# A four-layer graph network: sorted edge scopes addressed by one packed register, and fewer of them in the first streamed layer

## What is computed

```python
h = jnp.maximum(_layernorm(x), 0.0)
x = x + segment_sum(relu(concat(h[dst], h[src], ea32) @ W1 + b1) @ W2 + b2, dst)       # layer 0
h = jnp.maximum(_layernorm(x), 0.0)
x = x + elu(segment_sum(h[src] * softmax_over_dst(edge_weight1), dst))                 # layer 1
h = jnp.maximum(_layernorm(x), 0.0)
x = x + segment_max((h[dst] - h[src]) @ theta.T + theta_b + (h @ phi.T + phi_b)[src], dst)  # layer 2
h = jnp.maximum(_layernorm(x), 0.0)
x = x + x_plus_mean_of_mlp3(concat(h[src], h[dst], ea16), dst)                         # layer 3, three matrices
```

## Time and profile before

| | |
|---|---|
| median of 3 runs | 7997.08 us (7992.33 to 8004.19) |
| profiled execution, its own time | 8001.27 us |
| its span | 7999.5 us, 104510 instructions |
| busy share of the span | PE 80%, PEld 60%, DVE 72%, ACT 46%, POOL 66% |
| gathers of layer 1, first to last start | 2145.2 to 3927.2 us |
| gathers of layer 2, first to last start | 4091.6 to 5812.1 us |

### The profile page before, as it was taken

The page is one execution under the profiler, slowest core; times in us unless marked ns, Lnnn a source line. Parts: engine busy times, 40 slices in busy tenths (PEclk is TensorE's granted clock), DMA queues, the critical chain, the costliest instruction groups (busy, mean ns, idle before and its releaser), DMA issues.

```text
span 7999.5 us, 104510 instructions
## 1 busy us (share of the span) xinstructions
PE 6388.0 (80%) x31092; PEld 4821.3 (60%) x31092; DVE 5739.1 (72%) x7826; ACT 3705.8 (46%) x7759; POOL 5280.6 (66%) x5553
## 2 busy tenths in 40 slices
PE   0899999998588887787568887777705999999995
PEld 0677777776566665565446665555503667676674
DVE  6888888887688877777678885555555777777773
ACT  5144344444266665556545553333302555555552
POOL 7777777777655555555557774444467777777776
PEclk9999999999688888878779997777757999999996
DMA  8466666665344444444325553333313555555553
GB/s 313 105 168 158 155 156 154 156 156 148 80 117 118 118 116 104 103 104 104 73 77 137 135 132 91 87 86 89 83 36 88 142 142 144 143 143 142 144 143 83
DMA packets 1091448, 994.96 MB, mean 124 GB/s; under 512 B 582060, under 2 KB 828234, under 8 KB 1090794
## 3 DMA queue, kind: packets, MB, share of 16 engines
q1 hardware_dynamic: 895326, 788.45, 33.7%
q0 software_dynamic: 178896, 157.24, 13.2%
q10 hardware_dynamic: 16700, 42.58, 1.4%
HBM read 621.46 MB, written 366.24 MB: 123 GB/s over the span
## 4 chain that ended last, share of the span: by engine, by line
PE 42%; POOL 12%; issue 12%; DVE 5%; DMA 2%; ACT 0%; SPq 0%; POOLq 0%; DVEq 0%; ACTq 0%
PE pScope L1197 23%; POOL G L826 8%; PE pScope L1189 5%; PE pScope L1121 4%; DVE sorted_rows L1715 4%; PE pEven L1214 3%; POOL R L847 2%; DMA G<-table,idx 2%; PE pEven L1295 2%; PE pT L1281 1%; POOL R_hidden L847 1%; POOL first_rows L787 1%; PE pScope L1314 1%; PE pScope L1302 1%; PE pEven L1302 1%
## 5 line engine op out<-in xcount | busy, mean ns | idle before, releaser
L826 POOL DMA_INDIRECT G<-table,idx x2770 | 2614.2, 944 | 848.3 <-issue 814.4
L826 POOL DMA_INDIRECT G<-table,e_dst x2084 | 1973.5, 947 | 1568.9 <-DVE S L1757 954.2
L1197 PE MATMUL pScope<-h_high,slot_onehot 128*128 x3406 | 1587.0, 466 | 144.3 <-issue 138.5
L1620 DVE TENSOR_TENSOR_SCAN K<-mask_f,K,pT 48x512 f32<-48x512 bf16 x782 | 1005.3, 1286 | 765.0 <-PE pT L1281 617.0
L1197 PE MATMUL pScope<-h_low,slot_onehot 128*128 x3406 | 1456.7, 428 | 0.0
L955 ACT ACTIVATE K<-pT 48x512 f32<-48x512 f32 x782 | 460.9, 590 | 1546.2 <-PE pT L1281 1539.0
L1715 DVE TENSOR_REDUCE sorted_rows<-pScope 128x192 f32<-128x1920 f32 x262 | 563.6, 2151 | 750.2 <-PE pScope L1203 750.1
L1197 PEld LDWEIGHTS pScope<-h_high,slot_onehot 128*128 128x128 f32 x3406 | 759.4, 223 | 473.9 <-issue 351.8
L1001 ACT ACTIVATE rows_split<-sorted_rows 128x192 fp32r<-128x192 f32 x262 | 95.0, 363 | 1638.7 <-DVE sorted_rows L1715 1638.7
L1197 PEld LDWEIGHTS pScope<-h_low,slot_onehot 128*128 128x128 f32 x3406 | 757.5, 222 | 118.4
L1189 PE MATMUL pScope<-unchosen_sorted,minus_big 128*128 128x480 fp8e4 x1048 | 363.3, 485 | 569.7 <-issue 478.3
(11 more groups left out here) (274 smaller groups left out, 11703.1 us busy)
## 6 DMA issues: line engine op xcount, KB each, us to landing
prefix<-O_hidden SPq DMA_DIRECT2D x390, 512.0 KB
mask_f<-slot_rows SPq DMA_DIRECT2D x262, 416.0 KB, 3.6
mask_f<-same_row SPq DMA_DIRECT2D x392, 256.0 KB, 3.4
prefix<-O SPq DMA_DIRECT2D x194, 512.0 KB, 4.8
G<-first_rows SPq DMA_DIRECT2D x784, 96.0 KB
mask_f<-place_rows SPq DMA_DIRECT2D x262, 256.0 KB, 3.6
G<-table,idx POOLq DMA_INDIRECT x2770
first_rows<-zeros ACTq DMA_DIRECT2D x14, 2688.0 KB, 16.2
```

What stands on the lines that cost most here:

```text
L826: pool.indirect_dma_start(rows[:, slot, j, 0:widths[l]], None, table[l], bass.IndirectOffsetOnAxis(ap=at[:, n, j:j + 1], axis=0))\
L1197: pe.matmul(scope_sum[:, bass.ds(bank, SPAN * D)], slot_onehot[:, k % 2, slot, :], part[:, bass.ds(row, SPAN * D)], start=False, stop=False)
L1620: dve.tensor_tensor_scan(K[r, c.slot, :], mask_of(c, r), pT[c.slot % 2][r, :], K[r, (c.slot - 1) % RING, CHUNK - 1:CHUNK], ALU.mult, ALU.add)\
```

## The change

**Counts.** In layer 1 only column 3 of each half is a scope: 98. In layer 2 column 2 is one as well in halves whose number leaves 2 when divided by 3: 130. `LAYER_SCOPES` maps a layer's k-th scope to its number in the sort. 130 scopes are sorted, 6 of them ahead of layer 1, the others with the 98 sums of layer 1, none to two at a sum (`SORTS`).

**Register.** The tiles of the 11 middle slots, two bits each, are packed in one number per scope (the first slot is always tile 0, the last one tile 3). `load_tiles` loads it into one register, for scope k+1 right after the sum of scope k; for each slot PE shifts and masks it and computes both addresses.

**Two halves.** DVE reduces tiles 0 and 1, then tiles 2 and 3, and raises `rows_reduced` after each. PE hides and fills tiles 0 and 1 for slots 0 and 1 after the first, and goes on after the second.

**Order.** In DVE's step the scope's work (reduction, low half, hiding, marking, sort, place) stands ahead of the stream's transposes and scans. ACT weights the duo after the next. SP stores slot rows at the step of the place. The first two scopes of a layer are turned right after their sums and placed two steps earlier.

**Between the layers.** ACT copies the products to `h_high` too; DVE's cast goes, and its subtraction is made in two parts, behind the marking of scope 0.

```diff
-EXTRA_HALVES = (3, (1,))
+EXTRA_HALVES = {1: (1, ()), 2: (3, (2,))}
-SORT_LEAD = 5
+SORT_LEAD = 6
-SLOT_GROUPS = ((0, 4), (4, 8), (8, 13))
+TURNED_AT_ONCE = 2
...
-    SLOTS_LOAD, MARK, PLACES_LOAD, COPY_SLOTS, REDUCE, SPLIT, PLACE = 13, 9, 7, 6, 4, 3, 0
+    SLOTS_LOAD, MARK, PLACES_LOAD, REDUCE, SPLIT, PLACE = 13, 9, 7, 4, 3, 0
+    SORT_AT, EARLY_PLACE = (5, 3, 1), 2
...
-        slot_regs = over("sort_span end", "e_dst", "slot_regs", [P, SORT_SETS, SLOTS, 2], i32)
+        slot_regs = over("sort_span end", "e_dst", "slot_regs", [P, SORT_SETS], i32)
...
+                    act.activation(h_high[:, bs, :][:, first:stop, :], made[:, :, 0, :], ACT.Copy).then_inc(hq_copied, 1)
...
-                        if l == 1 and step >= 0 and step % 2 == 0:
-                            weight_rows(step // 2)
+                        if l == 1 and step % 2 == 0 and 0 <= step // 2 + 1 < DUOS:
+                            weight_rows(step // 2 + 1)
...
+            def load_tiles(l, k):
+
+                scope = LAYER_SCOPES[l][k]
+                tiles = pe.alloc_register(f"tiles{l}_{k}")
+                pe.reg_load(tiles, slot_regs[scope % SORT_ROWS:scope % SORT_ROWS + 1, scope // SORT_ROWS:scope // SORT_ROWS + 1])
+                return tiles
+
+            def tile_of(tiles, l, k, slot):
+
+                if slot in (0, SLOTS - 1):
+                    return (SCOPE - 1) * (slot > 0)
+                tile = pe.alloc_register(f"tile{l}_{k}_{slot}")
+                pe.reg_alu(tile, tiles, 2 * (SLOTS - 2 - slot), ALU.logical_shift_right)
+                pe.reg_alu(tile, tile, SCOPE - 1, ALU.bitwise_and)
+                return pe.snap(tile, donate=True, min_val=max(0, slot - PICK_GROUPS + 1), max_val=min(SCOPE - 1, slot))
...
+                    for part in h_parts:
+                        pe.matmul(scope_sum[:, bass.ds(tile * CHUNK, SPAN * D)], slot_onehot[:, k % 2, slot, :],
+                                  part[:, bass.ds(slot * SPAN * D - tile * (SPAN * D), SPAN * D)], start=False, stop=False)
...
                 if k:
-                    pe.wait_ge(rows_reduced, SCOPES_BEFORE[l] + k)
...
+                    pe.wait_ge(rows_reduced, 2 * before_k - 1)
+                hide(range(0, 2))
+                for slot in range(2):
+                    add_slot(slot)
+                if k:
+                    pe.wait_ge(rows_reduced, 2 * before_k)
+                hide(range(2, SCOPE))
+                for slot in range(2, SLOTS):
+                    add_slot(slot)
...
-                for k in range(NSC + 1):
-                    if k < NSC:
-                        sum_scope(l, k)
-                    if k >= 1:
+                tiles = load_tiles(l, 0)
+                for k in range(SCOPE_COUNT[l]):
+                    sum_scope(l, k, tiles)
+                    if k + 1 < SCOPE_COUNT[l]:
+                        tiles = load_tiles(l, k + 1)
...
+                    if k < TURNED_AT_ONCE:
+                        turn_scope(l, k)
+                    elif k > TURNED_AT_ONCE:
                         turn_scope(l, k - 1)
...
-                    dve.tensor_reduce(sorted_rows[:, :, :], pScope[:, :, 0:SPAN * D].rearrange("p t (b d) -> p t d b", d=D),
-                                      AX, ALU.max).then_inc(rows_reduced, 1)
+                    for ts in (slice(0, 2), slice(2, SCOPE)):
+                        dve.tensor_reduce(sorted_rows[:, ts, :], pScope[:, ts, 0:SPAN * D].rearrange("p t (b d) -> p t d b", d=D),
+                                          AX, ALU.max).then_inc(rows_reduced, 1)
...
+                    for bs, q in ((slice(0, B - 2 * NODE_BLOCKS), NQ - 2), (slice(B - 2 * NODE_BLOCKS, B), NQ)):
+                        dve.wait_ge(hq_stored, 16 * q)
+                        dve.wait_ge(hq_copied, 6 * q)
+                        last = dve.tensor_tensor(h_low[:, bs, :], hq[:, bs, :], h_high[:, bs, :].bitcast(f32), ALU.subtract)
...
+                        for k in scopes_at(l, step, REDUCE):
+                            reduce_rows(k)
+                        for k in scopes_at(l, step, SPLIT):
+                            keep_low(k)
...
+                        for k in scopes_at(l, step, PLACE, EARLY_PLACE):
+                            place_scope(k)
                         d, odd = divmod(step, 2)
                         if not odd and 0 <= d - 2 < DUOS:
                             turn_out(d - 2)
```

More of the change, by code:

```diff
@@ L131, in build @@
     HID = L0_W1.shape[1]
-    SCOPES = stream_scopes(HALVES)
+    SCOPES = stream_scopes(2, HALVES)
+    LAYER_SCOPES = {l: [SCOPES.index(scope) for scope in stream_scopes(l, HALVES)] for l in (1, 2)}
+    SCOPE_COUNT = {l: len(LAYER_SCOPES[l]) for l in (1, 2)}
     NSC = len(SCOPES)
@@ L153, in chunks_of, with scopes_at, scopes_until @@
         return range(2 * d, min(2 * d + 2, NCH))
[L155 to L165, removed]
-    SLOTS_LOAD, MARK, PLACES_LOAD, COPY_SLOTS, REDUCE, SPLIT, PLACE = 13, 9, 7, 6, 4, 3, 0
+    PLACE_AT = {1: [], 2: []}
+    for l, at in PLACE_AT.items():
+        for k, scope in enumerate(LAYER_SCOPES[l]):
+            half = SCOPES[scope][0]
+            at.append(max(k * 2 * DUOS // SCOPE_COUNT[l] - 3, CH * (half - 1), *(last + SCOPE_STEPS for last in at[-1:])))
+            assert at[k] <= CH * half - (3 if l == 1 else 1)
+    def scopes_at(l, step, lag, early=0):
+        return [k for k, at in enumerate(PLACE_AT[l]) if at - lag - (early if k < TURNED_AT_ONCE else 0) == step]
+    def scopes_until(l, half):
+        return sum(SCOPES[scope][0] <= half for scope in LAYER_SCOPES[l])
+    SORTED_UNTIL = [min(NSC, SORT_LEAD + k * NSC // SCOPE_COUNT[1]) for k in range(SCOPE_COUNT[1])] + [NSC]
+    SORTS = [range(*pair) for pair in zip(SORTED_UNTIL, SORTED_UNTIL[1:])]
+    assert all(len(sorts) <= 2 for sorts in SORTS)
+    SLOTS_LOAD, MARK, PLACES_LOAD, REDUCE, SPLIT, PLACE = 13, 9, 7, 4, 3, 0
+    SORT_AT, EARLY_PLACE = (5, 3, 1), 2
+    for k, sorts in enumerate(SORTS):
+        loads = [PLACE_AT[1][i] - SLOTS_LOAD for i, scope in enumerate(LAYER_SCOPES[1]) if scope in sorts]
+        assert all(PLACE_AT[1][k] - PLACE <= load for load in loads)
     MARKED_EARLY = {1: 2, 2: 1}
@@ L516, in gathers_of @@
                 return [j for j in range(TJ) if j != PICK_COLUMN]
-            return [j for j in range(TJ) if not (l in STREAMED and (n // CH, j) in SCOPES)]
+            return [j for j in range(TJ) if not (l in STREAMED and (n // CH, j) in [SCOPES[scope] for scope in LAYER_SCOPES[l]])]
         def ring_count(l, k):
-            before_l = sum(i % 2 == k % 2 for i in range(NSC)) if l == 2 else 0
+            before_l = sum(i % 2 == k % 2 for i in range(SCOPE_COUNT[1])) if l == 2 else 0
             return 16 * (before_l + k // 2 + 1)
@@ L1179, in sum_scope @@
-            def sum_scope(l, k):
-                pe.wait_ge(scope_marked, SCOPES_BEFORE[l] + k + 1)
-                if k:
-                    pe.wait_ge(rows_reduced, SCOPES_BEFORE[l] + k)
-                if l == 1:
-                    pe.wait_ge(spans_hidden, k + 1)
-                groups = iter(SLOT_GROUPS)
-                ahead = slot_addresses(l, k, next(groups))
-                for t in range(SCOPE):
-                    pe.matmul(pScope[:, t, 0:SPAN * D], minus_big[:, :],
-                              unchosen_sorted[:, k, t, :].rearrange("p (s o) -> p s o", o=1).to_broadcast([P, SPAN, D]),
-                              start=True, stop=False)
-                slot = 0
-                while slot < SLOTS:
-                    addresses = ahead
-                    for i, (row, bank) in enumerate(addresses):
-                        for part in h_parts:
-                            pe.matmul(scope_sum[:, bass.ds(bank, SPAN * D)], slot_onehot[:, k % 2, slot, :],
-                                      part[:, bass.ds(row, SPAN * D)], start=False, stop=False)
-                        slot += 1
-                        if i == 0 and slot + len(addresses) - 1 < SLOTS:
-                            ahead = slot_addresses(l, k, next(groups))
@@ L1952 @@
     src4 = np.concatenate([src4, np.zeros((P, E // CHUNK - chunks, TJ), src.dtype)], 1)
-    sorts = np.concatenate([src4[:, half * CH:half * CH + SCOPE, j] for half, j in stream_scopes(E // GROUP)], 1)
+    sorts = np.concatenate([src4[:, half * CH:half * CH + SCOPE, j] for half, j in stream_scopes(2, E // GROUP)], 1)
     rows = src[:chunks * CHUNK].reshape(-1, P, TJ)
```

124 lines of the change are left out of this document (65 added, 59 removed).

## The result

| | before | changed | forecast |
|---|---|---|---|
| median | 7997.0 us | 7661.15 us (7653.07 to 7670.23) | 7350 (7285 to 7530) |
| ratio to before, 95% interval | | 0.958 (0.9563 to 0.9596) | 0.919 |
| layer 1, first to last gather | 1782.0 us | 1796.0 us | 1498 |
| layer 2, first to last gather | 1720.5 us | 1377.4 us | 1355 |

Layer 2 gave nearly what it should, 343 us of 366. Layer 1, forecast to give 285, lost 14. Nothing else moved by more than 5 us: 1782.0 + 1720.5 - 1796.0 - 1377.4 = 329 of the 339 by which the span fell (7999.5 to 7660.2).

A forecast was written before the change was run, and what follows sets the result against it. POOL, kept waiting for DVE's scans, was to become the bound in both streamed layers: 8001.3 - 285 (layer 1) - 366 (layer 2) + 2.9 + 0.6 = 7354, put at 7350 for the median, range 7285 to 7530.

The forecast's parts named there:

- the early weighting: Layer 1, ACT's queue: waiting for gathers 7.5 us later was costed at nothing, covered by 15 us before the scope's place.
- B: Rival, layer 1: a half keeps its 16.9 us, 175 us more, total 7525; chance 0.13.
- that rival's first half: Layer 1 keeps 16.9 us a half because DVE, ACT and PE wait on each other in turn; B's chance 0.13.
- B's signs: Layer 1: a half above 15.5 us with long waits of DVE on ACT or PE, or a clock below 0.9.
- B's second half: Layer 1: PE, idle a third of each half, falls to 1.2 GHz each time; B's chance 0.13.
- Layer 1's slack per engine: Layer 1, a half: DVE needs 11.9 us, ACT under 11.6, PE 10.9, all under POOL's 15.0, so POOL bounds.
- The start: Layer 2: POOL's stand for the first scan, 27.6 us before, shrinks by 5 to 23.
- the first turns: Layer starts: turning the first two scopes right after their sums lies inside the start stalls, -3 to +3 us.
- The arithmetic: PE's queue: shift, mask and two addresses for 11 of 13 slots hide behind the matmuls and cost nothing.
- rival A: PE's register arithmetic shows in part: a slot takes 0.60 us instead of 0.435, total 7461; chance 0.12.
- D: Rival: late scopes wait for the register table's second set, not the register count; 214 us more, 7564; chance 0.06.
- Sorting ahead: Between layers: one more sort ahead of layer 1 costs 2.9 us, nothing if layer 0's tail covers it.

The follow-up runs named there:

- x1: The changed kernel with ACT's early weighting in layer 1 undone (duo d instead of d+1): 7363.28 us, ratio to before 0.9213.
- x4: The changed kernel with all 130 sorts ahead of layer 1 and none in its stream: 7814.36 us, ratio to before 0.9778.
- x8: x1 with the first two scopes of a layer turned behind the next scope's sum and placed at their ordinary step: 7334.48 us.
- x13: x8 with 26 registers a scope in three loads from the padded table of x12 and no register arithmetic: 7292.82 us.
- x7: The kernel before, with scopes 66 to 130 also reading registers from the table's first set, so the output is wrong: 7516.62 us.
- x12: The kernel before with its register table padded from 13 to 16 slots a set, so the second set begins at 128 bytes: 7510.51 us.

## Why the prediction was wrong, step by step

- **The step that failed** is the early weighting: "a scope is placed two duos, 15 us, after its reduction, so I cost this at nothing". I had looked only at what the scope of the same step needs, and had seen that its high halves and marks queue behind the wait. I hadn't followed the slot copies behind it to DVE, where the change puts the hiding that waits for them early in the step, ahead of marks, sort, place and scan, and from the scan back to the gathers that ACT waits for. In place of nothing, x1 shows 298 us, 296 of them in layer 1. Nor did the 15 us cover the part that I had seen: with the sorts gone, some 95 us of loss stayed in x4, where PE's turn waits for the marks.
- **Its price.** The text had said that B is what it costs if the cover is gone, and that rival's first half, engines that wait for each other in turn, is what happened. B's signs came as written: a half above 15.5 us, long waits of DVE for ACT and a clock below 0.9; POOL waited over 200 us for scans as well. Its price was wrong: I let layer 1 keep 16.9 us a half, while a new loop has a length of its own, 1796 / 98 = 18.3 on average. 7661 lies above 7525 and above the range.
- **B's second half** fell as a cause by itself: the clock was 0.75 in the changed layer 1, and at 0.83 in x1 POOL was the bound. It may have a share in the loop all the same, for the turn in the timeline above took 3.63 us against 1.97 in the earlier trace rows; no run takes that share apart. The rule cited from the Trainium skill ("TensorE: Matmul & The Clock Gate", section "HAM oscillation") describes PE there rightly: it waits between bursts, and the granted clock is 0.75.
- **The rest of the sum came out, in part by luck.** With nothing for the early weighting the sum was 7350; with that weighting undone, x1 measured 7363, 0.2% off. But layer 2 took 16 us more there than forecast, and the time between the two layers' gathers and behind them 14 us less than before (164.4 to 158.3 and 2187.4 to 2179.6), where the sum had next to nothing. Within layer 1's 1500.1 against 1498 the first wait took 26.0 us where the sum had 17.
- **Layer 1's slack per engine** (DVE 11.9, ACT under 11.6, PE 10.9 against POOL's 15.0) was right: in x1, at 1500.1 / 98 = 15.3 us a half, the stretch shown gives DVE 12.2, ACT 9.9 and PE 11.5, and POOL sets the pace.
- **Layer 2** was forecast at 1355 and took 1377.4. Two terms were too small. The start, put at 23 us, was 39.5 for the first wait: I took -3 to +3 for the first turns, and in x8 they measured 21 us here and 19 in layer 1. With them undone the stage is 1351.3. The arithmetic, put at nothing, is 0.67 - 0.435 = 0.23 us a slot, in some seven slots of a scope: rival A's mechanism, above its 0.165 a slot but on fewer slots. The sum had PE at 9.3 us a scope, below POOL's 10.05; PE is busy 99%, at 10.2 us a scope (4312.74 - 4302.52 from one closing pair to the next), just above POOL's 10.05, so the arithmetic hardly shows in the time: layer 2 is 19 us shorter in x13 than in x8.
- **The loads.** I took the 0.8 and 3.1 us before the hide as the price of loading 26 registers, with the second set somehow dearer. The 3.1 is not the usual wait: of 58 late scopes of the kernel before (4780 to 5700 us), three in four start their hide 2.1 to 2.3 us behind the reduction and every fourth 3.0 to 3.3, the one of the earlier trace rows among them. The scope ahead of it, where 5001.24 - 4999.06 = 2.18:

```profile
4996.90 2.16 DVE L1715 TENSOR_REDUCE sorted_rows<-pScope 128x192 f32<-128x1920 f32 x1 [6.14 <-PE pScope L1203]
5001.24 1.76 PE L1189 MATMUL pScope<-unchosen_sorted,minus_big 128*128 128x480 fp8e4 x4 [2.56 <-issue]
```

  Why every fourth, no run shows. It is the place of the loads that counts, and not their number: D's guess, that the second set is the slow one, was right as far as the kernel before goes (x7, x12), and D fell as a rival since the load of one register, 4 bytes into its row, shows no wait. Whether it is fast there or only covered, no run takes apart. The rule of about 200 ns a register from the Trainium skill ("Runtime: NRT & Kernel Launch", section "Instruction fetch mechanics") is given there for registers loaded from HBM, while these come from on-chip memory. Taken for them all the same, it would give 26 registers the same price in both sets; x12 against before shows that they differ, by 482 us over both layers.
- **Sorting ahead** at 2.9 us each was right (2.88 in x4). Between the layers 5 us went (164.4 to 159.4), the lower end of the -5 to +3 given there, where the sum had +0.6. Nothing else of the smaller parts shows.

## What to carry to other kernels

Before you move a wait up in an in-order queue, list what now stands behind it. Go on from each of these to the queue where somebody waits for it, and see whether you come back to what the wait itself waits for. If so, the length of that loop is a bound, whatever the busy shares say. When a stretch is slow from one index on, test what changes there with the index, the place of the data first, before the work is designed anew: a padded table gave here more than a new addressing scheme.

## What the runs showed of the hardware

- **Where a load of several registers begins.** PE loads a scope's registers from a row in on-chip memory in three loads, and the first, of 8 registers, stands between reduction and hide. Where the three begin 0, 32 and 64 bytes behind the table's start, the hide starts 0.8 us behind the reduction; at 104, 136 and 168 bytes 2.2 us, and 3.0 to 3.3 in every fourth scope; at 128, 160 and 192 bytes 0.8 again (x12). The table itself begins at a multiple of 32 bytes. Whether 32, 16 or another step is the one that counts, or a border that a load crosses, wasn't tried. A load of one register at 4 bytes, the changed kernel's second set, shows no wait: the turn behind it in PE's queue starts 0.12 us after the closing products begin (4904.72 and 4904.84), and in the changed layer 2 the clock is 1.00 and POOL issues 393 operations in 500 us, early as late.
- **Register arithmetic in PE's queue.** With four to six register operations between pairs of products, by a count in the program, the pairs start 0.67 us apart, 0.23 more than without; with two they start as close as with fixed addresses.
